# A routing stage written out pass by pass, its statistics ahead of a wait, its padding scatters amid the last pass

## What is computed

```python
h = layernorm(x) * (1 + cb) + sb
scores = h @ router                                  # 4096 tokens x 8 experts
topv, topi = top_k(scores, 2)
gates = sigmoid(scores, and 0 where not among the two)
for e in 8 experts:
    r = h * gates[:, e]
    out += (silu(r @ w_in[e]) * (r @ w_sw[e])) @ w_out[e]
out += (silu(h @ shared_in.T) * (h @ shared_sw.T)) @ shared_out.T
x = x + gb * out
```

## Time and profile before

| | us |
|---|---|
| runs shown, median of 3 | 3681.88 (3681.81 to 3682.46) |
| profiled execution | 3681.08 |
| its span, first to last instruction | 3679.3 |
| PE busy | 3321.7 |
| DVE busy | 1945.8 |
| ACT busy | 1564.9 |
| POOL busy | 567.7 |
| mean granted clock of TensorE | 0.955 |
| routing stage | 595 to 889 of the span |

### The profile page before, as it was taken

The page is one execution under the profiler, slowest core; times in us unless marked ns, Lnnn a source line. Parts: engine busy times, 40 slices in busy tenths (PEclk is TensorE's granted clock), DMA queues, the critical chain, the costliest instruction groups (busy, mean ns, idle before and its releaser), DMA issues. The chain is left out here.

```text
span 3679.3 us, 47577 instructions
## 1 busy us (share of the span) xinstructions
PE 3321.7 (90%) x16112; PEld 1955.1 (53%) x16113; DVE 1945.8 (53%) x4733; ACT 1564.9 (43%) x3481; POOL 567.7 (15%) x591
## 2 busy tenths in 40 slices
PE   5999996785999969999998899998899899997998
PEld 3455554453666644444443566666445566665454
DVE  1999994332111125555553677776331677775332
ACT  1766662220222215555554565665221456554211
POOL 0000001543000048100000322221000211111112
PEclk8999997887999979999999999999899999998999
DMA  3000003102111121000000100000000100000000
GB/s 128 1 1 1 1 1 121 46 23 97 46 46 46 44 60 55 9 1 1 1 1 1 60 10 10 9 8 5 24 0 1 36 8 10 9 8 5 12 12 23
DMA packets 72640, 90.19 MB, mean 25 GB/s; under 512 B 10975, under 2 KB 61427, under 8 KB 72179
## 3 DMA queue, kind: packets, MB, share of 16 engines
q1 hardware_dynamic: 65186, 69.28, 5.7%
q0 software_dynamic: 7248, 18.26, 1.6%
HBM read 59.63 MB, written 24.12 MB: 23 GB/s over the span
## 5 line engine op out<-in xcount | busy, mean ns | idle before, releaser
L1602 DVE CUSTOM_DVE_ANT_0 sb_win_masked<-ps_win_pss,sb_win_around 128x384 f32<-128x384 f32 (+1 forms) x512 | 255.7, 538 | 229.7 <-PE ps_win_pss L1709 229.7
L2010 ACT ACTIVATE sb_loc_pr<-ps_loc_psw,sb_loc_nb,sb_loc_sc 128x256 f32<-128x256 f32 x512 | 281.0, 568 | 187.8 <-DVE sb_loc_nb L2137 187.8
L2213 PE MATMUL ps_loc_psa<-sb_stk_w,sb_loc_hT 128*128 128x512 f32 x768 | 350.8, 607 | 4.9 <-DMA sb_stk_wo<-in_loc_wo 3.2
L2500 PE MATMUL ps_mlp_ps<-sb_mlp_hT,sb_stk_w 128*128 128x512 f32 (+1 forms) x768 | 322.7, 613 | 22.3 <-DVE sb_mlp_hid L2453 22.3
L1527 ACT ACTIVATE sb_win_pT<-ps_win_pst 128x512 f32<-128x512 f32 x368 | 199.7, 595 | 207.0 <-PE ps_win_pst L1720 205.4
L2213 PEld LDWEIGHTS ps_loc_psa<-sb_stk_w,sb_loc_hT 128*128 128x128 f32 x768 | 142.2, 192 | 181.8 <-issue 178.3
L2500 PEld LDWEIGHTS ps_mlp_ps<-sb_mlp_hT,sb_stk_w 128*128 128x128 f32 (+1 forms) x768 | 130.1, 184 | 201.7 <-issue 201.7
L719 PE MATMUL ps_rec_psp<-sb_rec_hT,sb_rec_w 128*128 128x512 f32 x512 | 235.7, 604 | 1.0 <-ACT sb_rec_hT L422 1.0
L2453 DVE SCALAR_TENSOR_TENSOR sb_mlp_hid<-ps_mlp_ps,sb_stk_col,sb_mlp_gl 128x512 f32<-128x512 f32 x96 | 71.7, 750 | 303.4 <-ACT sb_mlp_gl L2422 303.4
L2422 ACT ACTIVATE sb_mlp_gl<-ps_mlp_ps,sb_stk_col 128x512 f32<-128x512 f32 x96 | 65.9, 687 | 381.8 <-PE ps_mlp_ps L2500 381.6
L1709 PE MATMUL ps_win_pss<-sb_win_kT,sb_win_q 32*128 32x384 f32 (+1 forms) x1024 | 223.4, 518 | 4.7 <-DVE sb_win_top L1602 3.0
(11 more groups left out here) (316 smaller groups left out, 6552.8 us busy)
## 6 DMA issues: line engine op xcount, KB each, us to landing
sb_exp_rows<-sorted_tokens SPq DMA_DIRECT2D x72, 128.0 KB, 2.0
expert_results<-sb_exp_res SPq DMA_DIRECT2D x72, 128.0 KB, 1.7
sb_keep_x<-in_x SPq DMA_DIRECT2D x1, 4096.0 KB, 22.8
sb_moe_w_in<-in_L_ffn_w_in_eDF SPq DMA_DIRECT2D x8, 512.0 KB, 11.3
sb_moe_w_sw<-in_L_ffn_w_swiglu_eDF SPq DMA_DIRECT2D x8, 512.0 KB, 11.4
sb_exp_w_out<-in_L_ffn_w_out_eFD SPq DMA_DIRECT2D x8, 512.0 KB, 7.6
sb_stk_angles<-in_angles SPq DMA_DIRECT2D x32, 128.0 KB, 3.8
out_y<-sb_stk_y SPq DMA_DIRECT2D x8, 512.0 KB, 2.9
```

What stands on the lines that cost most here:

```text
L1602: i = nc.vector.tensor_tensor_reduce(masked[:, pair % 2, j, 0:keys], pss[:, (n + j) % PLAIN, 0:keys], around[:, first:first + keys], 1.0, ...
L2010: e = nc.scalar.activation(pr[:, hf, h], psw[:, hf, h // 2, h % 2 * 256:h % 2 * 256 + 256], ACT.Exp, scale=sc8[:, b, hh:hh + 1], bias=nb[: ...
L2213: t = nc.tensor.matmul(psa[:, c], hT[:, b, k, 1 - k:P + 1 - k], w[:, k, c * 512:(c + 1) * 512], start=(k == 0), stop=(k == KD - 1))
L2500: i = nc.tensor.matmul(ps[at:at + M, q % 2, i2], w1[:, k, i2 * HID + f * P:i2 * HID + f * P + M], hT[:, b, k], start=(k == 0), stop=(k == ...
```

## The change

It touches `route_tokens` alone.

- The three shared weights get a semaphore of their own, `s_shared`; `s_w` keeps the six small loads. DVE does `normalise(0)` ahead of its two memsets and its wait, PE its transposes ahead of its waits. PE waits for `s_shared` in pass 0 behind the router product, before up(0). POOL waits for `s_ones` and no longer for the loads.
- All four engines' passes are written out (`for it in range(NBLK)`), no hardware loop is left in the stage, and slices by `it` are constants.
- `og` becomes [128, 2, 4, 256], a half for each batch; output(b) waits for the x-add of the same batch in the pass before. DVE's wait for the x-adds at the end of each pass goes; one is left at the stage's end.
- In the last pass DVE computes the pads' rows and the first four table operations behind product(4), the next nine before output(0), the last nine before output(1).
- In the last pass POOL issues the eight pad scatters behind the 16 row scatters, waiting for all of these to have landed, and does the two x-adds behind them.

The diff, with the moved table operations left out where they are unchanged:

```diff
@@ -852,7 +852,7 @@
         gated = m.sb("gated", [P, TI, 2, D])
         act_f = m.sb("act_f", [P, 2, BLK])
         hid = m.sb("hid", [P, 2, KF, BLK])
-        og = m.sb("og", [P, TB, D])
+        og = m.sb("og", [P, NB, TB, D])
         settle = m.sb("settle1", [P, 1])
         padf = m.sb("padf", [P, EXP])
         padu = m.sb("padu", [P, EXP], U32)
@@ -872,9 +872,9 @@
         psr = psg
         pst = m.ps("pst", [P, BLK])
         s_b, s_sorted, s_padded = (t["soft"][n] for n in ("before_in", "sorted", "padded"))
-        names = ("w_load ones score scorecp top topi topf pick chosen es es1 gate rank run place placed rowf rowu row "
+        names = ("w_load shared_load ones score scorecp top topi topf pick chosen es es1 gate rank run place placed rowf rowu row "
                  "hmul h gated pair silu hid out og xadd pad padzero table settle")
-        (s_w, s_ones, s_score, s_scorecp, s_top, s_topi, s_topf, s_pick, s_chosen, s_es, s_es1, s_gate, s_rank, s_run,
+        (s_w, s_shared, s_ones, s_score, s_scorecp, s_top, s_topi, s_topf, s_pick, s_chosen, s_es, s_es1, s_gate, s_rank, s_run,
          s_place, s_placed, s_rowf, s_rowu, s_row, s_hmul, s_h, s_gated, s_pair, s_silu, s_hid, s_out, s_og, s_x,
          s_pad, s_padzero, s_table, s_settle) = (m.sem(n) for n in names.split())
         ROUTED = TI * 2
@@ -888,9 +888,9 @@
                 sp.dma_start(iota[:], a["iota"]).then_inc(s_w, 16)
                 sp.dma_start(steps[:], on_all(a["steps"], SEQ * NB // P)).then_inc(s_w, 16)
                 sp.dma_start(block_no[:], a["block_no"].unsqueeze(0)).then_inc(s_w, 16)
-                sp.dma_start(w_in[:, EXP], a["shared_in"].rearrange("(k p) f -> p k f", p=P)).then_inc(s_w, 16)
-                sp.dma_start(w_sw[:, EXP], a["shared_sw"].rearrange("(k p) f -> p k f", p=P)).then_inc(s_w, 16)
-                sp.dma_start(w_out[:], a["shared_out"].rearrange("(k p) d -> p k d", p=P)).then_inc(s_w, 16)
+                sp.dma_start(w_in[:, EXP], a["shared_in"].rearrange("(k p) f -> p k f", p=P)).then_inc(s_shared, 16)
+                sp.dma_start(w_sw[:, EXP], a["shared_sw"].rearrange("(k p) f -> p k f", p=P)).then_inc(s_shared, 16)
+                sp.dma_start(w_out[:], a["shared_out"].rearrange("(k p) d -> p k d", p=P)).then_inc(s_shared, 16)
 
                 for e in range(EXP):
                     for dst, name in ((w_in, "L0_ffn_w_in_eDF"), (w_sw, "L0_ffn_w_swiglu_eDF")):
@@ -904,8 +904,8 @@
             @block.gpsimd
             def _(pool):
                 pool.dma_start(before[:], a["before"]).then_inc(s_b, 16)
-                pool.wait_ge(s_w, 16 * 9)
-                with pool.Fori(0, NBLK) as it:
+                pool.wait_ge(s_ones, 3)
+                for it in range(NBLK):
                     for b in range(NB):
                         u = it * NB + b + 1
 
@@ -926,16 +926,17 @@
                             pool.indirect_dma_start(t["sorted"], bass.IndirectOffsetOnAxis(ap=rowu[:, n, c:c + 1], axis=0),
                                                     gated[:, n, c], None).then_inc(s_sorted, 16)
                     pool.wait_ge(s_settle, it + 1)
+                    if it == NBLK - 1:
+                        pool.wait_ge(s_pad, 2)
+                        pool.wait_ge(s_sorted, NBLK * ROUTED * 16)
+                        for e in range(EXP):
+                            pool.indirect_dma_start(t["sorted"], bass.IndirectOffsetOnAxis(ap=padu[:, e:e + 1], axis=0),
+                                                    zeros[:], None).then_inc(s_padded, 16)
                     for b in range(NB):
                         pool.wait_ge(s_og, it * NB + b + 1)
-                        xt = x[:, bass.ds(it * TB + b * TPB, TB)]
-                        nc.gpsimd.tensor_tensor(xt, xt, og[:], ALU.add).then_inc(s_x, 1)
-                pool.wait_ge(s_pad, 2)
-                pool.wait_ge(s_sorted, NBLK * ROUTED * 16)
-                for e in range(EXP):
-                    pool.indirect_dma_start(t["sorted"], bass.IndirectOffsetOnAxis(ap=padu[:, e:e + 1], axis=0),
-                                            zeros[:], None).then_inc(s_padded, 16)
+                        xt = x[:, it * TB + b * TPB:it * TB + b * TPB + TB]
+                        nc.gpsimd.tensor_tensor(xt, xt, og[:, b], ALU.add).then_inc(s_x, 1)
                 pool.wait_ge(s_padded, EXP * 16)
                 pool.wait_ge(s_padzero, 16)
 
@@ -964,15 +965,69 @@
                                 for k in range(KD):
                                     norm.affine_chunk(act, it + 1, b, k, pst[:])
 
-                blocks_ahead(act, step)
+                for it in range(NBLK):
+                    step(it, it + 1 < NBLK)
 
             @block.vector
             def _(dve):
+                norm.normalise(dve, 0)
                 nc.vector.memset(ones[:], 1.0).then_inc(s_ones, 1)
                 nc.vector.memset(zeros[:], 0.0).then_inc(s_ones, 2)
-                dve.wait_ge(s_w, 16 * 9)
+                dve.wait_ge(s_w, 16 * 6)
                 nc.vector.tensor_copy(run[:], region[:]).then_inc(s_run, 1)
-                norm.normalise(dve, 0)
+                n_table = [0]
...
+                def pads():
+                    dve.wait_ge(s_run, NBLK + 1)
+                    nc.vector.tensor_scalar(padf[:], run[:], iota[:, 0:1], None, ALU.add).then_inc(s_pad, 1)
+                    dve.wait_ge(s_pad, 1)
+                    nc.vector.tensor_copy(padu[:], padf[:]).then_inc(s_pad, 1)
+                def table_ends():
...
+                def table_blocks():
...
+                def table_rows():
...
 
                 def step(it, ahead):
                     u = it + 1
@@ -1012,9 +1067,9 @@
 
                     def output(b):
                         dve.wait_ge(s_out, it * NB + b + 1)
-                        if b:
-                            dve.wait_ge(s_x, it * NB + b)
-                        nc.vector.tensor_tensor(og[:], pso[:], keep["gates"][:, 0, 1, b:b + 1].broadcast_to([P, TB, D]),
+                        if it:
+                            dve.wait_ge(s_x, (it - 1) * NB + b + 1)
+                        nc.vector.tensor_tensor(og[:, b], pso[:], keep["gates"][:, 0, 1, b:b + 1].broadcast_to([P, TB, D]),
                                                 ALU.mult).then_inc(s_og, 1)
 
                     product(0)
@@ -1037,7 +1092,7 @@
                     product(3)
                     dve.wait_ge(s_rowf, u)
                     nc.vector.tensor_copy(rowu[:], rowf[:]).then_inc(s_rowu, 1)
-                    nc.vector.tensor_copy(rows[:, bass.ds(it, 1)], rowf[:].unsqueeze(1)).then_inc(s_row, 1)
+                    nc.vector.tensor_copy(rows[:, it:it + 1], rowf[:].unsqueeze(1)).then_inc(s_row, 1)
                     dve.wait_ge(s_gate, u)
                     dve.wait_ge(s_h, it * NB + NB)
                     for n in range(TI):
@@ -1046,9 +1101,14 @@
                                                         None, ALU.mult)
                     i.then_inc(s_gated, 1)
                     product(KF)
+                    if not ahead:
+                        pads()
+                        table_ends()
                     product(KF + 1)
                     if ahead:
                         norm.statistics(dve, it + 1)
+                    else:
+                        table_blocks()
                     output(0)
                     product(KF + 2)
                     if ahead:
@@ -1058,68 +1118,22 @@
                     product(KF + 3)
                     if ahead:
                         norm.scale_rows(dve, it + 1, 1, ahead=True)
+                    else:
+                        table_rows()
                     output(1)
-                    dve.wait_ge(s_x, it * NB + NB)
 
                     dve.wait_ge(s_sorted, it * ROUTED * 16 + ROUTED * 16)
 
-                blocks_ahead(dve, step)
-                dve.wait_ge(s_run, NBLK + 1)
-                nc.vector.tensor_scalar(padf[:], run[:], iota[:, 0:1], None, ALU.add).then_inc(s_pad, 1)
-                dve.wait_ge(s_pad, 1)
-                nc.vector.tensor_copy(padu[:], padf[:]).then_inc(s_pad, 1)
...
+                for it in range(NBLK):
+                    step(it, it + 1 < NBLK)
+                dve.wait_ge(s_x, NBLK * NB)
 
             @block.tensor
             def _(pe):
-                pe.wait_ge(s_w, 16 * 9)
+                norm.transpose(pe, 0, lambda b, k: ps[:, b, k])
+                pe.wait_ge(s_w, 16 * 6)
                 pe.wait_ge(s_ones, 1)
                 pe.wait_ge(s_b, 16)
-                norm.transpose(pe, 0, lambda b, k: ps[:, b, k])
 
                 def step(it, ahead):
                     for b in range(NB):
@@ -1171,6 +1185,8 @@
                                                      skip_group_check=True)
                         i.then_inc(s_out, 1)
 
+                    if it == 0:
+                        pe.wait_ge(s_shared, 16 * 3)
                     for q in range(UF):
                         up(q)
```

(51 more changed lines are left out.)

36 lines of the change are left out of this document (16 added, 20 removed).

## The result

The changed kernel took 3663.61 us (median of 4 runs, 3660.82 to 3664.85) against 3682.17 for the kernel before beside it; the ratio is 0.9949, 95% interval 0.9936 to 0.9961. So it is 18.6 us faster, where 46.5 were forecast; the time lies in the range of 3626 to 3674, nearer to case B (3668) than to the forecast of 3635. Its profiled execution has a span of 3661.8 us, 17.5 less than before.

The account below looks back on a forecast made before the run. TensorE, busy for 90% of the span, was taken as the bound, so only its work and gaps count; −10.1 − 0.8 − 32.7 − 2.9 = −46.5 from 3681.08 gave 3634.6, forecast as 3635 us, range 3626 to 3674.

Parts of the forecast that it names:

- case B: Rival: the lag stays, belonging to the ahead work beside the scatters; −13.8 us, 3668 us; chance 0.31.
- The start: Stage's start: normalise(0) ahead of DVE's wait for loads moves everything behind it earlier; −10.1 us, bounds −8 and −10.5.
- the late signals: First three passes: writing out the loop ends silu(7)'s 8.3 us lag behind up(7) and the clock's drop; −32.7 us.
- The loop's issue: Three pass boundaries: semaphores and branch, 0.3 us each on PE, go with the loop; −0.8 us, bounds 0 and −2.
- og for each batch: output(1) waits for batch 1's x-add a pass ago; the removed wait ends nothing today; 0 us.
- The pads and the table: Stage's tail: pads directly behind row scatters, table operations hidden in the last pass; −2.9 us, bounds 0 and −5.5.
- D: Rival: lag stays and a fetch of written-out code lands while the routed weights load; 3679 us; chance 0.07.
- E: Rival: slower, as fetches of written-out code stand in PE's and DVE's path in several places; 3690.7 us; chance 0.04.

Follow-up runs that it names:

- set 2: Runs on one chip where nothing was late: kernel before 3647.5 us, changed kernel 3634.06 us, ratio 0.9961.
- set 3: Runs on one chip where signals were late: kernel before 3681.2 us; changed kernel 3661.23; changed kernel with statistics, deviation and scaling early 3647.04.
- sets 1 and 3: Two sets of runs, each on one chip, with late signals; the kernel before took 3672.2 us in the first and 3681.2 us in the other.
- set 4: Runs on one chip where nothing was late: kernel before 3647.2 us, changed kernel 3635.52, kernel before with only its passes written out 3643.52.

## Why the prediction was right and where it was wrong

**The start: right.** −10.1 holds in every trace but one: up(0) is 15.5 to 15.6 us behind the statistics with and without the change. In the first trace of the changed kernel it is −13.4; the 3.3 more are nearly all the clock, which rose within the router product there and not in the others. That was luck of one execution and no merit of the forecast. `s_shared` and the small loads ended nothing, as worked out.

**The step that failed** is the 32.7 us for the late signals. The prediction took what one profiled execution showed as the program's, and gave it to the loop, because the loop was one of two differences to the fourth pass. The loop is not the cause: without it silu(7) is still 6.8 to 7.5 us late. And the lag is no fixed property of the program: the kernel before has none of it in set 2.

The prediction also misread a row that was before it. It took ACT's idle time until silu(6) for a sign that the work for the next pass was not the cause. But up(6) had ended long before:

```profile
783.40 1.88 PE L1141 MATMUL ps_route_ps<-sb_route_hT,sb_moe_w_sw 128*128 128x512 f32 x4
```

That is 785.28, and silu(6) starts at 789.92: it was itself 4.6 us late, though the view names the product as its releaser. Down(0)'s signal to og(0) is late as well, by 3.1 us in that pass.

What was found in the loop's place is work beside POOL's scatters. In the first three passes 17 instructions of DVE for the statistics, 6 of ACT and 10 of DVE for the scaling stand there, and behind them PE's turns; the fourth pass of the kernel before had none of these. Moving the 17 away put silu(7) in time; moving ACT's 6 as well gained nothing more. All of it together, with the 10 put at the scatters' beginning, gained 14 us over the changed kernel in set 3; what the 10 have of that isn't known, as no set with late signals has the runs with and without it. In each of these runs of sets 1 and 3 a turn's signal stayed late, by up to 4 us. Adding 16 short copies on ACT cost 7 and 8 us, while 3 of equal duration cost nothing. So on ACT it is the number of instructions (or how close they follow each other) that counts and not the busy time. For DVE that is inferred: no run put fewer, longer operations in place of the 17, so their number and their use of the SBUF beside POOL are not told apart.

Nor is the number all. With the change the fourth pass has 24 table operations beside its scatters, 15 of them ahead of silu(6), and silu(6) and silu(7) are in time; only og(1), behind the last nine, starts 2.0 us late (down(1) ends at 843.82, og(1) at 845.90), which it did not before. The pads hide it. So "A loss is excluded, as the fourth pass shows what written-out code does here" had a wrong ground: that pass lacked what makes signals late.

Of the 32.7 us the changed kernel got some 3 to 5 (the first three passes above are 6.1 shorter behind up(0), of which the loop's issue is 1 to 3). The loops alone gained 9.7 us in the set with late signals and 3.7 in one without. That a loop's branch and register instructions count among the instructions beside the scatters would explain the difference; it is only argued, and the intervals of the two gains meet at about 7 us, so the difference itself is barely shown.

**The lag itself was real and rightly priced.** Where nothing is late, the passes of before take 54.0 to 55.5 us, where 53.7 were worked out, the stage is 33 us shorter, where 32.7 were, and the whole kernel takes 3647. But what brings it is not the change.

**The loop's issue: too small.** −0.8 was forecast. (Three times the 0.3 that it was taken from are 0.9.) By the traces of set 2 it is −3.1 from the first router product to og(1), beyond the bound of −2; the trace of the loops alone in set 4 has the same 211.4 us there as the changed kernel in set 2, against 214.5 for the kernel before. What takes the 3.1 is not known.

**og for each batch: 0, as forecast.** PE and DVE wait for the same things as before.

**The pads and the table: right in kind, −1.7 and not −2.9.** The wait for the row scatters' landing is 2.26 us and not 1.5, the last row scatter starts some 0.5 later than before against up(7), and the clears behind the x-adds take 0.3 more. The eight pad scatters take 9.9 us and not 10.2, which gives 0.3 back. The rule of the Trainium skill (SBUF — State Buffer, "two separate sides"), by which descriptors wait for VectorE's two-port operations, would, by an estimate from the two figures of that page, have added some 2.5 us for each table copy beside a scatter. The trace shows nothing of that size: the row scatters that ran beside the table's copies took 0.97 to 1.01 us, and the longest, 1.36 us where the median is 0.97, began at 823.31 beside two TENSOR_TENSORs of the table.

```profile
L926 POOL DMA_INDIRECT sorted_tokens<-sb_route_gated,sb_route_rowu x64: 965/969/1360, 631.1 to 840.4; - x64
```

**Rivals.** B, with −13.8, is what happened in its terms: 3668 forecast, 3663.6 measured, and 13.4 where nothing is late. That its sum comes so close is partly luck: the passes gave 2.3 us more than its 0.8, the tail 1.2 less than its 2.9. D and E did not come. Code was fetched: 12 pieces on the two instruction queues q8 and q14 in the changed kernel's stage, 7 in that of the kernel before. But no pass of the written-out kernel is longer than before in its set by more than 0.6 us.

**What stays open** is what makes signals late. Two things go with it in every trace. It was in all traces of a set or in none of them; of what differs between sets the record has only the chip's number, and that was 10 in a set without late signals and in one with them. And where signals are late, the trace itself is incomplete in this stage, where none is late it isn't: in the clean executions each scatter's landing is known, in the others the view can't give it and often names releasers "remote". The same line of the kernel before, in set 2 and in the first trace (from the views of L926; the second has no line on landing):

```profile
L926 POOL DMA_INDIRECT sorted_tokens<-sb_route_gated,sb_route_rowu x64: 965/969/1063, 644.3 to 826.0; - x64
...
DMA to landing us min/median/max: 2.4/2.4/3.5
```

```profile
L926 POOL DMA_INDIRECT sorted_tokens<-sb_route_gated,sb_route_rowu x64: 965/969/1064, 644.1 to 858.0; - x64
```

Of the 323 semaphore updates that the engines' instructions make in this stage, the first trace of the kernel before lacks 25, that of set 2 none. All twelve traces with late signals lack 24 to 38, all eight without lack none. The two kinds of engine fare differently: 24 of the 25 are DVE's and ACT's, and the work behind them was in time all the same (ACT's Exp of the third pass starts at 779.70, the Ln that it waits for ends at 779.67, and there is no update between them in the trace), while PE's updates are nearly all there, and those of the late signals are recorded as late. So at least the record of events was crowded. A guess that would fit, and that no run shows, is one path for events that all engines share and that the scatters' completions and many short instructions fill. Whether it is the chip's signals that are crowded, or the recording of them that holds PE up, no experiment here could tell: every run on record has a span and a granted clock and so was recorded too.

## What to carry to other kernels

Before a large gap goes into a sum, see whether a second execution of the same program has it: here a term of 25 us with the same 8.3 us in three passes was there in some sets of runs and absent in others, for the same code. Subtract the product's end from the start of the work that waits for it, and don't go by the releaser's name: it was "remote" for silu(7) and the right product for silu(6), and both were late. Here it also paid to have few short instructions beside a burst of indirect DMAs: with the statistics of the next pass at its own head and the scaling right behind the gated rows (3633 us in set 2, 3647 in set 3) the kernel is as fast as the changed one where nothing is late and 14 us faster where something is.

## What the runs showed of the hardware that was not expected

The same program took 3647 us in two sets, 3672 in one and 3681 in two, as in the runs of the result (3682), and between the two executions of it that have a trace nearly all of the difference lies in one stage of 290 us. Sixteen one-element copies on ACT, 1.57 us in idle time, made PE's signals to ACT later and cost 7 to 8 us of the whole in one kind of set, and nothing in the other; three copies of together 1.64 us cost nothing in either. ACT, with nothing to wait for, stood 2.30 us behind them.
